# Attention with a folded feed-forward on one core: the first PV group of a batch moved next to the second one on TensorE

## What is computed

```python
y = layernorm(x, ln_w, ln_b)
q, k, v = (einsum('bsd,hde->bhse', y, w) for w in (wq, wk, wv))
scores = einsum('bhse,bhte->bhst', q, k) / sqrt(8) + causal
attn = einsum('bhst,bhte->bshe', softmax(scores), v).reshape(b, s, 128)
x1 = _layernorm(x + (attn @ wo + x))
x2 = _layernorm(x1 + x1 @ W.T + b + x1 @ lilora.T)      # lilora = up_aux @ lora_up @ lora_down @ down_aux
```

## Time and profile before

| what | value |
|---|---|
| median of 3 runs | 490.17 us (486.16 to 490.82) |
| the profiled execution | 489.89 us, of which the span from first to last instruction is 488.2 us |
| mean granted TensorE clock | 0.972 |
| busy share of the span | PE 90%, weight loads 69%, DVE 81%, ACT 72%, POOL 65% |
| instructions | 15362 |

### The profile page before, as it was taken

The page is one execution under the profiler, slowest core; times in us unless marked ns, Lnnn a source line. Parts: engine busy times, 40 slices in busy tenths (PEclk is TensorE's granted clock), DMA queues, the critical chain, the costliest instruction groups (busy, mean ns, idle before and its releaser), DMA issues.

```text
span 488.2 us, 15362 instructions
## 1 busy us (share of the span) xinstructions
PE 437.5 (90%) x5514; PEld 336.9 (69%) x5514; DVE 393.6 (81%) x1074; ACT 350.4 (72%) x867; POOL 315.9 (65%) x395
## 2 busy tenths in 40 slices
PE   0766989999999999899899999999999999998871
PEld 0545668777777777677787777777777777776541
DVE  2298867888888889799898999998899998987432
ACT  4213667778887778878787888888888888886842
POOL 8546874657766676656676766766666666755542
PEclk9996799999999999999999999999999999999995
DMA  2475266666665665766657566666777666661111
GB/s 78 123 169 133 66 163 148 160 155 152 159 168 148 160 169 136 175 175 152 174 129 181 151 158 163 163 157 157 173 174 174 160 154 153 155 157 46 31 38 33
DMA packets 70864, 69.21 MB, mean 142 GB/s; under 512 B 6955, under 2 KB 66146, under 8 KB 66146
## 3 DMA queue, kind: packets, MB, share of 16 engines
q1 hardware_dynamic: 70242, 68.48, 56.9%
q10 hardware_dynamic: 576, 0.13, 0.1%
HBM read 47.07 MB, written 20.99 MB: 139 GB/s over the span
## 4 chain that ended last, share of the span: by engine, by line
PE 56%; DMA 20%; DVE 7%; SPq 6%; issue 4%; POOL 4%; ACT 2%; POOLq 0%; ACTq 0%; DVEq 0%
DMA kx<-k_rows 15%; PE pv_bank L754 13%; PE score_bank L742 7%; PE bank L767 7%; PE bank L762 6%; PE max_bank L728 5%; PE max_bank L724 5%; DMA q_rows<-parts 4%; PE max_bank L729 4%; PE score_bank L743 4%; DVE rowmax L590 3%; PE bank L801 2%; SPq L300 2%; PE bank L802 2%; SPq L290 2%
## 5 line engine op out<-in xcount | busy, mean ns | idle before, releaser
L590 DVE TENSOR_REDUCE rowmax<-max_bank 128x2 f32<-128x512 f32 (+1 forms) x384 | 247.1, 676 | 32.0 <-PE max_bank L724 20.1
L421 ACT ACTIVATE probs<-score_bank 128x384 f32<-128x384 f32 x512 | 225.2, 491 | 50.1 <-PE score_bank L743 46.7
L391 POOL TENSOR_SCALAR_AFFINE_SELECT probs<-probs 128x1024 f32<-128x1024 f32 x128 | 140.9, 1101 | 81.5 <-ACT probs L421 81.5
L742 PE MATMUL score_bank<-qx,kx 74*128 74x256 bf16 x512 | 123.7, 276 | 0.5 <-ACT probs L421 0.4
L743 PE MATMUL score_bank<-qx,kx 74*128 74x128 bf16 x512 | 104.0, 220 | 0.0
L754 PE MATMUL pv_bank<-probs,v_ext 128*32 128x256 f32 (+1 forms) x2048 | 103.6, 331 | 0.0
L728 PE MATMUL max_bank<-kx,qx 128*128 128x128 bf16 x512 | 89.9, 227 | 5.5 <-DVE rowmax L590 5.3
L729 PE MATMUL max_bank<-kx,qx 74*128 74x128 bf16 x512 | 89.4, 226 | 0.0
L754 PEld LDWEIGHTS pv_bank<-probs,v_ext 128*32 128x32 f32 x2048 | 55.4, 109 | 34.9 <-issue 6.0
L728 PEld LDWEIGHTS max_bank<-kx,qx 128*128 128x128 bf16 x512 | 49.3, 100 | 26.2 <-DVE rowmax L590 16.6
L724 PE MATMUL max_bank<-kx,qx 128*128 128x128 bf16 x512 | 51.9, 226 | 13.7 <-DMA kx<-k_rows 13.4
(11 more groups left out here) (82 smaller groups left out, 614.5 us busy)
## 6 DMA issues: line engine op xcount, KB each, us to landing
kx<-k_rows SPq DMA_DIRECT2D x96, 192.0 KB
qx<-q_rows SPq DMA_DIRECT2D x64, 192.0 KB
qx<-q_rows SPq DMA_DIRECT2D x32, 208.0 KB
q_rows<-parts SPq DMA_DIRECT2D x32, 192.0 KB, 2.2
k_rows<-parts SPq DMA_DIRECT2D x32, 192.0 KB, 2.4
xa<-in_x SPq DMA_DIRECT2D x32, 128.0 KB, 4.8
k_rows<-parts SPq DMA_DIRECT2D x32, 128.0 KB, 2.3
xr<-in_x SPq DMA_DIRECT2D x32, 128.0 KB, 4.8
```

The source lines that it names most:

```text
L391: pool.affine_select(out=t, in_=t, compare_op=ALU.is_ge, fill=0.0, base=0, pattern=[[0, GROUP * NB], [1, P]], channel_multiplier=-1)\
L421: act.activation(probs[:, h, 0:PW], score_bank[SCORE_BANK[h]][:, 0:PW], ACT.Exp, scale=SCALE / Q_SCALE)\
L590: dve.tensor_reduce(to, of, AX.X, ALU.max).then_inc(s_mread[unit], 1)
L742: pe.matmul(b[:, 0:SEQ], k[0:SCORE_ROWS, i, 0:P], q[0:SCORE_ROWS, i, :], start=True, stop=True)
```

## The change

On TensorE, `pv(it, 1, 0)` is taken from behind `scores(it, 1, 8)` and put directly ahead of `pv(it, 1, 1)`. It moves past eight calls: `pv_transpose(it, 0, 1)`, `scores` 9 and 10, `max_transpose(it, 2)`, `max_scores(it, 3, 0)` and `(it, 3, 1)`, `scores` 11 and `feed_forward(it, -1)`, with the waits that stand among them. The other engines' streams are as before.

```diff
                 if it.runs(1):
                     scores(it, 1, 8)
-                    pv(it, 1, 0)
                 if it.runs(0):
                     pe.wait_ge(s_vx, it.done(4))
 ...
                     feed_forward(it, -1)
                 if it.runs(1):
+                    pv(it, 1, 0)
                     pv(it, 1, 1)
                 if it.runs(3):
                     max_scores(it, 3, 2)
```

## The result

The changed kernel takes 509.42 us (median of 4 runs, 507.15 to 515.59) against 490.5 us before: slower by a factor of 1.0385, 95% interval 1.0312 to 1.0459. The profiled execution took 508.15 us, its span is 506.4. Now and then an execution of either kernel is some per cent slower as a whole; the medians in this document take in all runs, the ratios leave such runs out.

The account below looks back on a forecast made before the run. The prediction took a TensorE, DVE and POOL cycle of 12.97 us a period as the bound. Terms of +7.8, +4.0, +1.5 and +1.5 us made +14.8 on 489.89 us, 504.7, stated as 504.5 us; range 497 to 511.

Parts of the forecast that it names:

- The bound: TensorE, DVE and POOL wait on each other in a 12.97 us cycle; TensorE's 90% matmul busy time is not the limit.
- the ring: L813 to unit 2 on DVE, 2.66 us, then DVE and POOL back to L813, 10.31 us: 12.97 us a period.
- The removal: Behind score 8, up to 0.88 us goes but gains nothing, becoming waits for the values' copy and for split_maxima.
- The addition: Group 0 ahead of group 1, between L813 and unit 2, has no cover: 0.65 us more a period, 13.62 us.
- The upper bound of 0.79: Cost in us of the added PV group if it takes as long as a single group; 0.65 was used instead.
- The transfers: Unit 0's eight waits for expanded keys, 98.96 to 274.02 us, fall from 6.7 us to some 2 us.
- Quiet stretch: 274 to 430 us, no transfer holding TensorE up: twelve periods at 0.65 us more each, +7.8 us.
- First part: 99 to 274 us: 13 periods of 13.62 us plus 2 us of waits, 179.1 against 175.06, +4.0 us.
- Start: 28 to 99 us, five periods also waiting for transfers: about 0.3 us each, +1.5 us.
- Drain: 430 to 488 us, the run's end: two or three such cycles, +1.5 us.
- main case: The whole kernel takes 500 to 507 us; chance 0.62.
- slower by more: Transfer waits don't shrink (510 us), or the added group costs 0.79 us (508 us): 507 to 513 us, chance 0.12.

Follow-up runs that it names:

- skip_group0: Kernel before with PV group 0 (16 matmuls a period) left out, so heads 0 to 3 are missing: 499.19 us, period 12.97 us.
- skip_group1: Kernel before with PV group 1 left out instead of group 0, so heads 4 to 7 are missing: 494.81 us, ratio 1.008, period 12.94 us.
- second trace: Each kernel profiled once more without any edit, single runs: changed kernel 505.5 us, kernel before 500.99 us; quiet periods 13.60 and 12.97 us.
- the filler: Changed kernel plus unread matmuls ahead of pv_transpose, 8 a period (14 in unrolled iterations): 501.62 us, ratio 1.0217 to the kernel before.
- group0_behind_max_transpose: Kernel before with PV group 0 moved to between max_transpose and unit 0 of max_scores, not beside group 1: 498.87 us, ratio 1.0146.
- skip_group1_other_bank: Kernel before without PV group 1 and with the transpose of attn in bank6 instead of bank7: 486.4 us, ratio 0.9902.

## Why the prediction was right, and where it was off

*The bound.* Right. TensorE's busy time looked like the limit, and leaving 16 of its matmuls out of each period changed the period by nothing (skip_group0). The room that the share of the weight loads, 78%, seemed to promise was small, though: with `shift_f` moved, TensorE's own order holds the period at 12.69 us, 0.28 less than before, with weight loads in flight for only 80% of it. Three engines close the ring, as the earlier trace rows had it. Incomplete was that I named one ring: by the rows there are three of nearly the same length, the others over the bank that `scale_ff` reads and over `normalize_x`. It did not matter for the forecast, since work was added; it would have spoilt a forecast for work removed, and did for skip_group1.

*The removal.* Right: nothing gained. The two waits are where they were placed, 0.47 us for the values and 0.27 for `split_maxima`.

*The addition.* Right. 0.65 us for the second group of a pair; L813 to unit 2 grew by 0.65 to 0.69 (2.22 to 2.87 and more), the period from 12.97 to 13.60 against 13.62 forecast. The upper bound of 0.79 holds for a group with a 128-column weight load behind it, and the pair has that seam already.

*The transfers.* Right in kind: the waits for the keys fell from 6.7 us in eight to 3.4 in five (3.2 in four in the second trace), forecast about 2.

*The sum, 14.8 us forecast against 18.2 us in the spans.* Quiet stretch: 7.8 forecast, 6.9 measured (the last period is short). First part: 4.0 against 6.4; of the difference some 1.7 us is what the two periods of 15.3 us lost beyond the stall of 1.6 us, at the low clock, and the rest is spread over other periods. Start: +1.5 against −1.6 (69.80 in place of 70.76 us, and 0.6 us earlier to begin with). Drain: +1.5 from 430 on against +6.5. That is the term that was mis-sized, in this pair of traces. The changed kernel's had two windows at the 1.2 GHz level, 454.8 to 461.6 us and 3.4 us more, ahead of its last 11 us, where the kernel before had none until its last 10 us. I had put nothing on the clock, from the middle stretches, where the earlier trace rows show 1.00, and had not looked at the drain, where TensorE has gaps anyway and the waits are longer (from the last score to L813 it is 1.12 us there, 0.60 before). With the filler, at full clock until its last 12 us, the drain is 60.2 us against 58.3, +1.9, near the forecast. How much of the +6.5 belongs to the change is open: in the second traces the drains are 62.9 and 60.4 us, +2.5, with low windows in both. The time, 509.42 us, is inside the range of 497 to 511, but above its main case of 500 to 507, where "slower by more" had been placed; the reasons given there did not come true, since the waits for transfers fell by half and the group cost 0.65.

*Open.* Why the start got shorter: it is 69.8 and 69.3 us in the two traces of the changed kernel, with low windows at the same places within 0.2 us, and 70.8 and 71.5 us in those of the kernel before, with others in each, and no run took this apart. Why the changed kernel and group0_behind_max_transpose, with the same quiet period, differ by 10 us in the total: the latter's trace has a drain of 59.7 us (438.87 to 498.5) and only one low window ahead of its last 10 us, but the two kernels were not timed side by side, and nothing here ties the pair to the drain.

## What to carry to other kernels

Where an engine is 99% busy and its neighbour waits too, look for a constant distance between a release and the instruction behind it: it marks a ring through several engines, and then the place of an instruction counts more than its cost. Work moved onto an arc of the longest ring costs its full price, work taken off it is worth only the distance to the next ring; so take work off the engine whose arc all rings share (here a small DVE instruction, put into DVE's idle slot). And cost the drain by itself, with its clock: in 11 of the 14 traces here the granted clock fell to the 1.2 GHz level between 440 and 470 us.

## What the runs showed of the hardware that was not expected

- `shift_f`, a DVE instruction on 2 elements a partition, is recorded with 565 ns (median of 32) behind `row_max` of unit 6 in the kernel before and with 150 ns behind `scale_ff` in the two kernels where it was moved, with the same operands. Why was not tried.
- The 1.2 GHz level came in the middle of dense work after a stall of 1.6 us (263.6) and of 1.3 us (236.4) in the changed kernel, but not after one of 1.4 us in the kernel before. In the changed kernel TensorE also waits 0.74 us in the 3 us ahead of the first of these stalls (0.47 for the values, 0.27 for `split_maxima`).
- Leaving work out made a kernel slower: skip_group1 does 16 matmuls less a period, keeps the period, and took 1.008 times as long (1.0031 to 1.0128). With one bank changed (skip_group1_other_bank) it took 0.9902 (0.9868 to 0.9937) on another chip, with the same period. The trace of skip_group1 has the low level at four places between 60 and 460 us. The kernel before has it at one in its first trace and at four in its second, so that the clock is the cause here is not shown.
